# Spreading 404 hosted network units anew over three stages of a graph network kernel, with one mark waiting for an older step

## The reference, cut to what matters

```python
x = ln(x + L0(x))   # edge softmax: alpha = softmax over receivers, sum of alpha * Wh[cols]
x = ln(x + L1(x))   # mean over neighbours, two dense products, relu, norm
x = ln(x + L2(x))   # convolution: per-edge weights from 10 edge scalars, messages, mean
x = ln(x + L3(x))   # attention:
    w_ij = mlp(edge_feats_64) + mlp(chi_scalar_32)      # silu(x @ w0 + b0) @ w1 + b1, width 256
    alpha = (q[receivers] * w_ij * k[senders]).sum(-1) / 4 * cutoffs
    out = segment_sum(alpha * v[senders], receivers) / 16
```

## Time and profile before

| | |
|---|---|
| Median of 3 runs | 9574.32 us (9573.35 to 9618.82) |
| Profiled execution, its own time | 9490.67 us |
| Span of the profiled execution | 9488.9 us |
| Mean granted TensorE clock | 0.896 |
| Busy share of the span | PE 81%, DVE 64%, ACT 54%, POOL 34% |

### The profile page before, as it was taken

One profiled execution on the slowest core, in us unless ns is written; L12 is line 12 of the kernel. 1 busy time (PEld: TensorE's weight loads), 2 busy tenths in 40 slices (PEclk: granted clock), 3 DMA queues, 4 the chain that ended last, 5 costly groups with the idle time before them and its releaser, 6 DMA issues. The chain is left out here.

```text
span 9488.9 us, 195846 instructions
## 1 busy us (share of the span) xinstructions
PE 7690.5 (81%) x51013; PEld 5812.3 (61%) x51014; DVE 6066.2 (64%) x12579; ACT 5138.6 (54%) x9232; POOL 3240.0 (34%) x3274
## 2 busy tenths in 40 slices
PE   5999999888699988888888888886777777766664
PEld 3656666677599975565666565664555555555453
DVE  7989998899844454555555555555555555555556
ACT  3666666788577764444444444445555555544442
POOL 0000000000000005555555555544555555555554
PEclk8999999999899998888888888898998999887775
DMA  3333333566466632222222222214555555454454
GB/s 113 137 134 137 136 139 136 182 226 223 154 182 183 182 107 57 59 58 59 57 59 58 58 59 56 59 50 139 156 154 148 160 155 153 144 152 145 142 146 115
DMA packets 627973, 1178.36 MB, mean 124 GB/s; under 512 B 215083, under 2 KB 288220, under 8 KB 608469
## 3 DMA queue, kind: packets, MB, share of 16 engines
q1 hardware_dynamic: 498618, 859.56, 28.6%
q0 software_dynamic: 129280, 317.93, 12.0%
HBM read 900.47 MB, written 276.57 MB: 124 GB/s over the span
## 5 line engine op out<-in xcount | busy, mean ns | idle before, releaser
L2257 POOL DMA_INDIRECT att_kv_rows<-kv_dram,att_stage x1616 | 1613.6, 999 | 1374.9 <-DVE att_msgs L2401 872.2
L2005 POOL DMA_INDIRECT conv_rows<-y_dram,conv_stage x1616 | 1559.2, 965 | 1225.0 <-DVE conv_msgs L2077 706.9
L851 PE MATMUL att_mlp<-mlp_w,mlp_hid 128*128 128x128 f32 x5088 | 758.8, 300 | 382.1 <-issue 318.9
L695 PE MATMUL conv_part<-conv_msgs,conv_hot 128*128 128x256 f32 x3232 | 896.7, 421 | 76.3 <-issue 75.9
L851 PEld LDWEIGHTS att_mlp<-mlp_w,mlp_hid 128*128 128x128 f32 x5088 | 686.0, 211 | 440.9 <-issue 374.4
L1974 ACT ACTIVATE conv_hid<-conv_hid_ps 100x512 f32<-100x512 f32 x408 | 243.3, 596 | 1172.7 <-DMA y_dram<-mean_nodes_both 807.7
L695 PEld LDWEIGHTS conv_part<-conv_msgs,conv_hot 128*128 128x128 f32 x3232 | 659.7, 215 | 189.3 <-issue 102.6
L2228 ACT ACTIVATE acc<-att_q_ps 128x512 f32<-128x512 f32 x404 | 239.2, 592 | 976.9 <-DMA kv_dram<-conv_nodes_qkv 644.2
L235 PE MATMUL count_ps<-count_cols,count_rows 128*128 128x392 bf16 x3920 | 730.1, 331 | 8.6 <-DVE count_cols L201 8.6
L695 PE MATMUL att_part<-att_msgs,att_hot 128*128 128x128 f32 x3232 | 571.9, 323 | 177.9 <-issue 127.9
L1047 PE MATMUL mean_sum_ps<-wh,mean_turned 128*128 128x129 f32 x4802 | 689.1, 283 | 9.3 <-DVE acc L1001 9.1
(11 more groups left out here) (276 smaller groups left out, 16321.4 us busy)
## 6 DMA issues: line engine op xcount, KB each, us to landing
c_dram<-count_counts SPq DMA_DIRECT2D x392, 392.0 KB, 2.4
mean_counts<-c_dram SPq DMA_DIRECT2D x343, 448.0 KB, 3.4
w_dram<-mlp_w SPq DMA_DIRECT2D x404, 256.0 KB
att_w_rows<-w_dram SPq DMA_DIRECT2D x404, 256.0 KB
soft_counts<-c_dram SPq DMA_DIRECT2D x98, 1024.0 KB, 4.8
mlp_feats<-in_feats SPq DMA_DIRECT2D x405, 192.0 KB
soft_counts<-c_dram SPq DMA_DIRECT2D x49, 1088.0 KB, 5.1
att_lanes<-lo_dram SPq DMA_DIRECT2D x404, 128.0 KB
```

The costliest lines, as they stand in the source:

```text
L695: ins = nc.tensor.matmul(part, c.hot[:, s, t, :], rows[:, t, :], start=half == 0 and t == 0, stop=half == 1 and t == T - 1)
L851: ins = nc.tensor.matmul(self.w_ps[:, t * D:(t + 1) * D], self.hid[:, n, t * P:(t + 1) * P], self.w1[:, n, :], start=n == 0, stop=n == 2 * ...
L2005: pool.indirect_dma_start(rows[:, s, t, :], None, y_dram, bass.IndirectOffsetOnAxis(ap=stage[:, s, t:t + 1], axis=0)).then_inc(gathered[s] ...
L2257: pool.indirect_dma_start(kv_rows[:, s, t, :], None, kv_dram, bass.IndirectOffsetOnAxis(ap=stage[:, s, t:t + 1], axis=0)).then_inc(gathere ...
```

## The change

The number of units of each stage changes, with how they are laid over a round. Counting hosts 2 a round (98), with one half of one unit in each window. Convolution hosts 2 a round in its first 10 rounds and 1 in the next 90 (110); its last round hosts none. Attention hosts 2 a round in 98 rounds (196) and none in the last 3. In attention's even bodies the four chunks of the first layer are split: chunks 0 and 1 run ahead of `sums` and chunks 2 and 3 after it. `columns` waits for `pick(g - 1)` where it waited for `pick(g + 1)`. SyncE's `stored` waits stand at five rounds, each for the units that the rounds up to the next one read.

```diff
-UB = 3
-COUNT_PAIR0, COUNT_PAIR1 = {0: 0, 3: 1, 5: 2}, {1: 0, 4: 1, 6: 2}
-COUNT_HALF0, COUNT_HALF1 = {2: 0, 5: 1, 7: 2}, {3: 0, 5: 1, 7: 2}
+UB = 2
+COUNT_PAIR0, COUNT_PAIR1 = {0: 0, 4: 1}, {1: 0, 5: 1}
+COUNT_HALF0, COUNT_HALF1 = {2: 0, 6: 1}, {3: 0, 7: 1}
...
-N_CONV = 98
-U_ATT = U_CONV + N_CONV
+CONV_TWOS, N_CONV = 10, 100
+U_ATT = U_CONV + CONV_TWOS + N_CONV
...
-                        if v in (4, 6):
-                            mlp.store(sp, u + v // 2 - 2)
-                        if v in (1, 4, 6):
-                            mlp.load_next(sp, u + v // 2 - (v > 1))
+                        if v == 4:
+                            mlp.store(sp, u)
+                        if v in (1, 5):
+                            mlp.load_next(sp, u + v // 4)
...
-                        if v in (4, 6):
-                            mlp.vector(nc, dve, UB * i + v // 2 - 2)
+                        if v == 4:
+                            mlp.vector(nc, dve, UB * i)
...
+        def unit_of(i, per):
+            return U_CONV + (2 * i if per == 2 else CONV_TWOS + i)
...
-                with pe.Fori(1, N_CONV) as i:
-                    body(i, False, True)
-                with pe.Fori(N_CONV, NI) as i:
-                    body(i, False, False)
+                with pe.Fori(1, CONV_TWOS) as i:
+                    body(i, False, 2)
+                with pe.Fori(CONV_TWOS, N_CONV) as i:
+                    body(i, False, 1)
+                body(N_CONV, False, 0)
...
-        twos, ones = 63, 96
-        assert U_ATT + 2 * twos + ones - twos == NG
+        twos = 98
+        assert U_ATT + 2 * twos == NG
...
-                with sp.Fori(1, 61) as i:
-                    body(i, 2, False)
-
-                mlp.stored(sp, U_ATT + 110)
...
+                rounds = [1, 52, 75, 88, 95, twos]
+                for r0, r1 in zip(rounds, rounds[1:]):
+                    if r0 > 1:
+
+                        mlp.stored(sp, S * r1 - 1)
+                    with sp.Fori(r0, r1) as i:
+                        body(i, 2, False)
...
                         pick_q_x(k, s)
+                        if per == 2 and s % 2 == 0:
+                            mlp.tensor_first(nc, pe, unit_of(i) + s // 2, range(2))
                         if s > 0:
                             sums(i, s - 1)
...
-                        if per:
-                            mlp.tensor_step(nc, pe, unit_of(i, per), s, per)
+                        if per == 2 and s % 2 == 0:
+                            mlp.tensor_first(nc, pe, unit_of(i) + s // 2, range(2, 4))
+                        elif per:
+                            mlp.tensor_step(nc, pe, unit_of(i), s, per)
...
-                    dve.wait_ge(q_done, g)
+                    dve.wait_ge(q_done, g - 2)
```

More of the change, by code:

```diff
@@ L1945, in _, with body @@
                     load_scalars(p, 2 * p)
-                def body(i, unit, first):
+                def body(i, per, first):
                     for s in range(S):
@@ L1954, in body @@
                             load_scalars(s // 2, S * (i + 1) + s - 1)
[L1955 to L1960 removed]
+                    if per:
+                        mlp.sync_body(sp, unit_of(i, per), per, first)
+                body(0, 2, True)
+                with sp.Fori(1, CONV_TWOS) as i:
+                    body(i, 2, False)
+                with sp.Fori(CONV_TWOS, N_CONV) as i:
+                    body(i, 1, False)
                 mlp.store(sp, U_ATT - 1)
[L1962 to L1963 removed]
+                body(N_CONV, 0, False)
                 mlp.finished(sp, U_ATT - 1)
@@ L1974, in silu, with body @@
                     nc.scalar.activation(hid[:, s], hid_ps[0:100], ACT.Silu, scale=10 ** -0.5).then_inc(hid_done, 1)
-                def body(i, unit, last=False):
+                def body(i, per, last=False):
                     for s in range(S):
@@ L2030, in turns, with body @@
                     lane_sums_x(nc, pe, c, s, 2 * i + s // 2, lambda t: msgs[:, s - 1 + t // T, t % T])
-                def body(i, early, unit):
+                def body(i, early, per):
                     for s in range(S):
@@ L2088, in add, with body @@
                     lane_add(nc, dve, c, s, S * i + s, k, Reach(dve, spans, k))
-                def body(i, first, unit):
+                def body(i, first, per):
                     for s in range(S):
@@ L2096, in body @@
                             add(i, 1)
-                        if unit and s == 1 and not first:
-                            mlp.vector(nc, dve, U_CONV + i - 1)
+                        if per and s == 1 and not first:
+                            mlp.vector(nc, dve, unit_of(i, per) - 1)
+                        elif per == 2 and s == 3:
+                            mlp.vector(nc, dve, unit_of(i, per))
                 dve.sem_inc(rows_used, S)
@@ L2241, in _ @@
                     body(i, 2)
-                with act.Fori(twos, ones) as i:
-                    body(i, 1)
-                with act.Fori(ones, NI - 1) as i:
+                with act.Fori(twos, NI - 1) as i:
                     body(i, 0)
@@ L2321, in _ @@
                     body(i, False, 2)
-                with pe.Fori(twos, ones) as i:
-                    body(i, False, 1)
-                with pe.Fori(ones, NI - 1) as i:
+                with pe.Fori(twos, NI - 1) as i:
                     body(i, False, 0)
@@ L2423, in _ @@
                     body(i, False, False, 2)
-                with dve.Fori(twos, ones) as i:
-                    body(i, False, False, 1)
                 mlp.vector(nc, dve, NG - 1)
-                with dve.Fori(ones, NI - 1) as i:
+                with dve.Fori(twos, NI - 1) as i:
                     body(i, False, False, 0)
```

58 lines of the change are left out of this document (23 added, 35 removed).

## The result

The change made the kernel slightly slower. After: 9657.56 us (median of 9 runs, 9630.15 to 9678.61); before, in the same comparison: 9592.99 (9 runs). The forecast was 9382, its range 9200 to 9515. The profiled execution after has a span of 9628.3 us, 139 us more than the one before.

A forecast was written before the change was run, and what follows sets the result against it. TensorE was taken to set the pace in counting and attention. Counting -108, convolution +62 and attention -145 summed to -191 us from 9490.67, so 9300, or 9382 on the median's scale; 8-in-10 range 9200 to 9515.

The forecast's parts named there:

- Counting: Counting's 49 rounds go from three units to two: VectorE becomes the bound, 33.55 to 31.35 us a round, -108 us.
- the lower bound of 30.84: Counting's round in us if the bias step and all of VectorE's wait for TensorE's sums go.
- rival E: Counting: TensorE's clock falls to attention's 0.74, +66 in place of -108, kernel 9557 us; chance 0.06.
- Convolution: Convolution hosts 12 more units, a second one in its first 10 rounds: +62 us, bounds +18 to +103.
- Attention, the split first layer: Attention: sums between the chunk pairs cover 2.1 us of silu wait, rounds 30.13 to 28.0 us; attention -145 us.
- The mark: Attention: VectorE's marks wait two picks further back; costed at 0, since VectorE does not set the pace.
- Thirty-three rounds from one unit to two: Attention: 33 rounds gain a second unit and go from 28.35 to 28.0 us, -12 us.
- B: Attention: the mark was the pace after all, rounds 26.2 us, total -368, kernel 9203 us; chance 0.16.
- C: Attention: something else sets a floor, two-unit rounds 29.2 us, total -74, kernel 9500 us; chance 0.24.
- D: Attention: the first pair's completion reaches ScalarE late, rounds 33.6 us, total +358, kernel 9935 us; chance 0.10.

The follow-up runs named there:

- conv_split: The changed kernel with the first-layer pairs split around the sums in convolution's ten two-unit rounds too; ratio to the kernel before 1.0051, those rounds 37.3 us.
- hosting: The changed kernel with attention's split and relaxed mark taken back, leaving only the units' new places; ratio to the kernel before 1.0010.
- split alone: The kernel before with the first layer's pairs split around the sums in attention's two-unit rounds, nothing else; ratio 1.0044, rounds 31.9 us.
- split_again: Repeat, in the fourth batch, of the kernel before with only attention's first-layer pairs split around the sums; ratio 1.0056.
- its control: The kernel before with VectorE's bias step of attention moved behind the next group's marks, the marks as they were; ratio 1.0017.
- mark_by_one: The kernel before with attention's mark waiting for the same group's pick, one step less relaxed than the change; ratio 1.0001 in a free batch.
- the slowest kernel: Fourth-batch repeat of the kernel before with the relaxed mark and SyncE's w rows loaded two groups ahead in attention; ratio 1.0186.

## Why the prediction was wrong

In the order of its own steps; the forecast summed to -191 before the scale, the ratio says +73.

**Counting, right, -137 for -108.** VectorE became the bound, with a round of 30.75 us for 31.35, just under the lower bound of 30.84. The clock stayed at 0.99, so rival E fell. The wait for the sums did not go whole, 2.02 us a round to 0.79; the bound was passed because other idle time of VectorE, which the sum left standing, shrank as well, 3.5 us a round to 1.5 in all.

**Convolution, undersized, about +104 for +62.** The place was right, the four chunks together (+103 was my upper bound, with two silu waits of 1.35 us). But TensorE's wait at the second pair is 8.1 us a round, 4 a unit, not 1.35: the completion of the first pair is held, as in the timeline. When a unit is hosted in quarters, the pairs stand in two bodies with the stage's own work between them, and the wait at line 842 is 0.15 us a round. Splitting the pairs inside the body did not help (conv_split).

**Attention, the split first layer: the step that failed, about +106 for -145.** Attention as a whole makes 251 of the 264 us of the error: the split was to save 2.1 us in each of its two-unit rounds, and of the +106 split and mark together are some +63 (1.0076 beside hosting's 1.0010) and the 33 rounds below most of the rest. I read 2.92 us a round of waiting for silu and took the part that the sums can cover as time saved. With plain loads the split does save, 1.0 us a round, half of the 2.1. With the gathers the same edit covers the wait (174.5 to 75.5 us for ScalarE in split alone) and saves nothing: split alone gave +0.44% and +0.56%. TensorE's idle time stayed at 8.1 us a round as it reappeared inside the second layer (3.9 us a round to 6.2), and its products took longer, at a granted clock of 0.85 in place of 0.90. The picks came later too, 3.0 us in the mean for split alone (2.8 in split_again) where hosting alone has 2.0. The sum charged idle time against the round one for one and let the busy time stand; neither held in a stage where completions come microseconds late. That the split's own order makes them later is what the numbers suggest; no run shows why.

**The mark, costed at 0, measured +1.34% and +1.35% alone.** The reason given, that VectorE's 6.4 us of waiting is slack, was true and beside the point. I asked what a faster VectorE gains, not what its earlier arrival changes. It costs nothing with plain loads and 1.3% with held completions. Earlier gathers are not the way (held back: 1.0154), and mending the late w rows gave nothing back (1.0186). It goes with a longer wait of VectorE's queue at line 868 and a lower clock of TensorE. That the one causes the other is argued, not shown, and 0.3 to 0.6% is left in the free condition without an explanation. In the whole change, split and mark together cost 1.0076 against hosting's 1.0010, 0.7%, less than the 1.8% of both alone; why they partly cancel stays open.

**Thirty-three rounds from one unit to two.** Costed at -12 because the split was to pay for them. Without it their rounds went from 28.6 us (29.1 in split alone, of the same batch) to 30.25 (hosting alone), +39 to +54. The difference of 1.78 us between two-unit and one-unit rounds was about the right price, 1.2 to 1.6 measured.

**The rivals.** B (attention at 26.2) and E did not come about. C had the right sign of doubt, that something else holds the rounds, and the wrong size: rounds of 29.2 were to be a floor, 30.8 came. D ended on the right side of no change, and its place was wrong: it wanted a wait at line 842 above 3.4 us a round in attention, and it fell to 2.7. D's mechanism is what the ten convolution rounds show. The earlier trace rows was the row that should have carried more weight: I used its 6.2 us to price one rival and not to doubt that a covered wait is a saved one. The forecast's own range was also added up wrong: its bounds for counting and convolution give 9312 to 9498, not 9300 to 9470. The Trainium skill, Perfetto Trace Analysis, "Tensor Engine Instruction", has the semaphore follow PSUM's acknowledgement and not the profiled end; the runs agree that the two differ, and show that the difference is 0.01 us or 1.98 us in the mean for the same picks, by what GpSimd issues beside them.

## What to carry to other kernels

Before a covered wait is booked as a gain, compare each completion's event with the recorded end of its instruction. Where an event is missing, take the start of the instruction that waits for it. Where the two lie microseconds apart, as here, a wait taken from one place may come back at another, and a relaxed wait can cost time on an engine that has slack. And read two traces against each other only if both kernels ran in one batch, or after a look at a stage that the edit leaves alone. Hosted work is best put where nothing delays completions, here counting, and spread there until the next engine is full.

## What the runs showed of the hardware

- While GpSimd issues gathers by index, completions of TensorE can come late, 1.98 us in the mean for a pick, over 1 us for 48% of them. Plain loads of the same bytes from the same engine: 0.01 us. Replacing the gathers of attention alone took 8.3% off this kernel's time.
- The delay has two conditions, for the same kernel and even the same chip: 9587.7 and then 8075.33 us. In the second the same gathers delay none of the picks whose event the trace has. It is the largest effect in this study, and nothing in the kernel set it. Only comparisons within a batch mean anything, and an experiment's ratio can depend on the condition: the mark cost 1.3% in held batches, and 0.6% beside its control in a free one.
- TensorE's granted clock in attention was 1.00 where completions were not held (mark_by_one), 0.90 before, 0.85 with the mark or the split alone and 0.81 in the slowest kernel, and the same products took 19.1, 22.3, 23.5 to 23.9 and 24.7 us a round.
